# Second layer's edge loop of a two-layer graph network: three small VectorE tensors held in PSUM instead of SBUF

## The reference, cut to what matters

```
W    = (w_comp @ weight.reshape(4, 128*128)).reshape(8, 128, 128)   # 8 types out of 4 bases
proj = einsum('ni,rio->nro', h, W)
msg  = proj[src, rel_type]
agg  = segment_sum(msg, dst)
out  = relu(h @ root_weight + agg + bias);   x = x + out
```

## Time and profile before

| | us |
|---|---|
| median of three runs | 10,770.8 |
| lowest, highest | 10,699.99, 10,827.0 |
| the profiled execution, its own time | 10,833.25 |
| its span, first to last instruction | 10,831.4 |
| PE busy, PEld busy | 6888.0, 5018.6 |
| DVE busy | 4208.4 |
| ACT busy | 958.8 |
| POOL busy | 6283.7 |

### The profile page before, as it was taken

One profiled execution on the slowest core, in us unless ns is written; L12 is line 12 of the kernel. 1 busy time (PEld: TensorE's weight loads), 2 busy tenths in 40 slices (PEclk: granted clock), 3 DMA queues, 4 the chain that ended last, 5 costly groups with the idle time before them and its releaser, 6 DMA issues. The chain is left out here.

```text
span 10831.4 us, 120635 instructions
## 1 busy us (share of the span) xinstructions
PE 6888.0 (64%) x29078; PEld 5018.6 (46%) x29078; DVE 4208.4 (39%) x8057; ACT 958.8 (9%) x1738; POOL 6283.7 (58%) x6284
## 2 busy tenths in 40 slices
PE   5777767777767776667774555565556555555555
PEld 3444444444444444444444444454445444444444
DVE  5444444444444444444453333333333333333333
ACT  2000000010001010001020000000000000000001
POOL 2555555555555555555526666666666666666664
PEclk8777777777777777777786777777777776777777
DMA  5222222222222222222231111111111111111112
GB/s 147 72 72 74 72 72 73 73 72 72 73 71 72 73 73 72 73 73 72 72 84 40 42 39 39 41 41 41 40 39 41 40 39 41 40 39 40 41 40 55
DMA packets 415233, 646.20 MB, mean 60 GB/s; under 512 B 128129, under 2 KB 232009, under 8 KB 414450
## 3 DMA queue, kind: packets, MB, share of 16 engines
q0 software_dynamic: 200704, 411.44, 15.1%
q1 hardware_dynamic: 214482, 234.24, 7.4%
HBM read 617.04 MB, written 28.13 MB: 60 GB/s over the span
## 5 line engine op out<-in xcount | busy, mean ns | idle before, releaser
L559 POOL DMA_INDIRECT G<-p_tab,idxs x3136 | 2981.5, 951 | 2466.7 <-DVE idxs L645 1489.3
L1063 POOL DMA_INDIRECT hT<-h_tab,idxs x3136 | 3300.6, 1052 | 1818.4 <-issue 907.8
L1080 PE MATMUL psA<-S,hT 128*128 128x256 f32 x6272 | 2099.9, 493 | 1811.1 <-DVE S L1150 897.0
L1080 PEld LDWEIGHTS psA<-S,hT 128*128 128x128 f32 x6272 | 1466.0, 246 | 2132.3 <-issue 1055.5
L587 PE MATMUL psM<-Z,w 128*128 128x512 f32 x1568 | 1139.9, 818 | 872.0 <-ACT Z L633 785.6
L662 DVE TENSOR_TENSOR_SCAN R<-mk,R,psM 128x512 f32<-128x512 bf16 x784 | 998.5, 1274 | 1734.2 <-issue 670.2
L1160 DVE TENSOR_TENSOR aggT<-psV,aggT 128x64 f32 x784 | 175.4, 224 | 3319.3 <-remote 1745.0
L603 PE MATMUL psE<-E,O 128*128 128x64 f32 x6272 | 1039.5, 322 | 401.1 <-DVE E L673 329.8
L1090 PEld LDWEIGHTS psV<-A,V 128*128 128x128 f32 x6272 | 1008.0, 231 | 578.2 <-issue 306.6
L1090 PE MATMUL psV<-A,V 128*128 128x64 f32 x6272 | 970.5, 308 | 439.4 <-issue 257.0
L603 PEld LDWEIGHTS psE<-E,O 128*128 128x128 f32 x6272 | 990.6, 240 | 472.3 <-DVE E L673 363.5
(11 more groups left out here) (86 smaller groups left out, 2506.6 us busy)
## 6 DMA issues: line engine op xcount, KB each, us to landing
mk<-marks SPq DMA_DIRECT2D x392, 256.0 KB
G<-p_tab,idxs POOLq DMA_INDIRECT x3136
pl<-marks SPq DMA_DIRECT2D x392, 128.0 KB
hT<-h_tab,idxs POOLq DMA_INDIRECT x3136
Qw<-q_tab SPq DMA_DIRECT2D x784, 32.0 KB
p_tab<-pq SPq DMA_DIRECT2D x14, 448.0 KB, 3.1
q_tab<-pq SPq DMA_DIRECT2D x14, 448.0 KB, 4.1
oh<-in_w SPq DMA_DIRECT2D x392, 4.0 KB
```

The lines of the kernel that those rows point to most:

```text
L559: pool.indirect_dma_start(G[:, s, j, :], None, p_tab, bass.IndirectOffsetOnAxis(ap=idxs[:, s, j:j + 1], axis=0)).then_inc(gathered[s], 16)
L1063: pool.indirect_dma_start(G[:, s, j, :], None, h2_tab, bass.IndirectOffsetOnAxis(ap=idxs[:, s, j:j + 1], axis=0)).then_inc(l1_gathered[s], 16)
L1080: ins = nc.tensor.matmul(psA[:, b, 0:NB * W], G[:, s, j, :], S[:, b, j, :, :].rearrange("p b w -> p (b w)"), start=j == 0, stop=j == GT - 1)
```

## The change

hot, thot and tprod are no longer SBUF tensors of their own. Two PSUM tensors of two banks each are added, so that all eight banks are taken. hot takes the first 256 columns of either bank of psH1, thot the 256 columns behind hot's first buffer, tprod the 1024 columns of psT1. No instruction, no wait and no loop is changed; shapes and types stay (32-bit).

```diff
-                thot = sb("thot", [P, TPI, NR], fp32)
-                tprod = sb("tprod", [P, TPI, NB, NR], fp32)
                 coef = sb("coef", [P, TPI, NB], fp32)
-                hot = sb("hot", [P, 2, GT, W], fp32)
                 S = sb("S", [P, 2, GT, NB, W], fp32)
...
                 psV = ps("psV1", [P, 2, 512])
+                psH = ps("psH1", [P, 2, 512])
+                psT = ps("psT1", [P, 1024])
+                assert GT * W + TPI * NR <= 512 and TPI * NB * NR <= 1024
+                hot = psH[:, :, 0:GT * W].rearrange("p b (j w) -> p b j w", j=GT)
+                thot = psH[:, 0, GT * W:GT * W + TPI * NR].rearrange("p (t r) -> p t r", r=NR)
+                tprod = psT[:, 0:TPI * NB * NR].rearrange("p (t b r) -> p t b r", b=NB, r=NR)
```

## The result

| | before | after |
|---|---|---|
| median, lowest to highest (12 runs each) | 10,770.11, 10,699.99 to 10,827.0 | 10,850.19, 10,835.09 to 10,869.61 |
| ratio after to before, 95% interval | | 1.0088 [1.0067, 1.0108] |
| span of the profiled execution | 10,831.4 | 10,848.1 |
| POOL busy | 6283.7 | 5945.7 |
| second loop in it, first to last of ACT's copies | 5132 | 5221 |

The kernel became slower by 0.9%, 80 us, although POOL has 338 us less to do. In the profiled executions the second loop is 89 us longer.

The account below looks back on a forecast made before the run. No engine fills the second loop: POOL needs 5.41 of 6.56 us a group and otherwise waits for the trailing chain. Profiled 10,833 less 130 gave 10,703, carried over to the runs' median as 10,640 us; range 10,450 to 10,850.

Parts of the forecast that it names:

- POOL's saving: Second loop: S no longer stretches gathers, their mean falls from 1052 to 951 ns, 317 us of POOL time saved.
- bounds 236 and 339: Least and most saving of POOL time in us: the stretch falls on hot as well, or all of it goes.
- priced at nothing: Second loop: hot, still with two SBUF inputs, was taken to add nothing to gathers above 951 ns.
- DVE: Second loop: PSUM operands leave DVE's times about unchanged; effect taken as 0, at most +-25 us.
- What arrives at the end: Second loop: of 317 us saved on POOL, 161 would arrive by the two rates; four fifths, 130 us, was taken.
- two fixed rates: Second loop: the chain passes a group per 7.65 us while POOL issues and per 3.77 us while it stands.
- Slower: Second loop: without S's pauses on POOL the trailing chain slows while POOL issues; 162 us more, 10,933; chance 0.16.
- the 8.3 us beyond which: Second loop: time per group while POOL issues above which the kernel would become slower, a group then costing over 6.51 us.
- The waits: Second loop: POOL's waits for psA and indices, 896 us before, were to become about 1080.
- three sums named beforehand: POOL's waits, second loop: about 1080 us for the forecast, 1210 if nothing arrives, under 900 if all arrives.
- Nothing arrives: Second loop: chain held up once per gather, so POOL's 317 us become stops; 10,771 us; chance 0.26.
- The first loop: It must not move; if it did, the comparison would not be of this change.

Follow-up runs that it names:

- e3: Kernel before with only coef, S's 128-column operand, moved to PSUM; hot, thot, tprod stay in SBUF: 10,963.52 us, 1.0104.
- e1: The change with only hot in PSUM, thot and tprod left in SBUF: 10,971.38 us, 1.0115 to the kernel before.
- e5: The change plus one 384-column POOL memset behind the fourth gather of each second-loop group: 10,690.19 us, 0.9938 to the kernel before.
- f2: The change plus one 384-column POOL memset per group, run again in another comparison: 10,707.34 us, 0.9964 to the kernel before.
- f4: The change plus 384-column POOL memsets behind the second and fourth gather of each group: 10,735.35 us, 0.9879 to the kernel before.
- e4: The change plus a 64-column POOL memset behind each gather of the second loop: 11,051.37 us, 1.0189 to the kernel before.
- x1: The change with the second loop's gathers replaced by POOL memsets to a scratch tensor: 8,463.63 us, beside 10,751.93 of the kernel before.
- x2: The change with the second loop's gathers replaced by SP's plain loads of as many rows, in order: 8,456.88 us, beside 10,751.93 before.
- f3: The change unaltered, run a third time in another comparison: 11,000.17 us, 1.0131 to the kernel before.
- f1: The change unaltered, run again in another comparison: 10,853.37 us, 1.0102 to the kernel before.
- e8: The change plus 384-column POOL memsets behind each group's second and fourth gather, beside a kernel before of 8,599.08 us: 8,738.88 us, 1.0162.
- x3: The change with only the first of each second-loop group's four gathers kept: 8,559.29 us, beside 10,862.99 of the kernel before.

## Why the prediction was wrong

- **POOL's saving: right.** 945 ns in place of a forecast 951, no gather held up by S, 336 us less (317 forecast, bounds 236 and 339). The rule of the Trainium skill (SBUF — State Buffer, Who interferes with whom) that an instruction of DVE with at most one SBUF input does not contend with GpSimd holds, and e3 adds that it holds with the smaller operand in PSUM too. The short instructions with two SBUF inputs hold gathers too, which the forecast priced at nothing. Under hot after the change 188 gathers start and take 966 ns in the mean. Under tprod 97 start: in e1 and e3 all are stretched (1109 ns), and after the change, with thot in PSUM, one is (945 ns in the mean). In the sum this is little.
- **DVE: right.** S 1224 ns, hot 427. The fixed cost of PSUM that the Trainium skill's page VectorE: DVE Perf Modes (The TRN2 errata) gives, by which S would be some 65 ns longer (an estimate from that page), does not show: 1225 and 1224 ns, and 8 ns on hot's write.
- **"What arrives at the end": the step that failed.** It took 7.65 us a group while POOL issues and 3.77 while it stands as two fixed rates, from which each microsecond of issuing saved has to bring something (130 us). Over the whole second loop before the change these rates are 7.56 and 3.97, so they were read rightly; after it they are 8.09 and 4.37, and a group costs 5.00 x (1 - 4.37/8.09) + 4.37 = 6.67 us (5221/784 = 6.66 measured) in place of the 6.31 forecast. The rate while issuing is no constant: after the change it is near 5 us a group for the first 10 us behind a break, then 35 and 14 us (0 copies in the 9.7 us shown). The stretched gathers, by the runs, were themselves breaks. Freed of them, POOL issues 16 gathers on end and has to stop behind each 16. The experiments show the sign: e1 and e3 take POOL's load off and are slower, e5, f2 and f4 give it back in pieces of 0.44 us and are faster. e4, in pieces of 0.17 us, is slower, so it takes a break of some length and not only load; from what length on, no run shows.
- **The rival "Slower": right in its mechanism, its size off.** Its words, the pauses that S forces are the only relief while POOL issues, are what e5 and f4 show. Its price of 162 us was twice the 80 us of the runs. It let a group take 9.18 us while POOL issues, and 8.09 were measured. That is also below the 8.3 us beyond which it was to be the slower case; the kernel was slower all the same, because the rate while POOL stands rose too, from 3.97 to 4.37, which the sum had held fixed.
- **The waits.** Of the three sums named beforehand, 1080, 1210 and under 900 us, none was met: 1262.9 + 47.8 = 1311, past the one at which nothing arrives. The rival "Nothing arrives" falls with that: a chain held up per gather, whatever the time between gathers, would not have run quicker in e5.
- **The Trainium skill's rule that PE and ACT never wait on anyone for SBUF** (SBUF — State Buffer, Who interferes with whom) was taken as speaking for "Nothing arrives". The runs don't contradict it: what comes late is the update of PE's work, and by x1 and x2 neither POOL's writes nor plain transfers slow the chain. No run shows what this rule of the Trainium skill says of SBUF itself.
- **The first loop** was not to move. In the profiles POOL's time in it moved by 72 us (5448 to 5376), and in f3's by 6, so it varies by as much from one execution to the next. The second loop grew in all (5132 before, 5221 after, 5209 in f1, 5297 in f3), which is the sign that was named for a wrong prediction.

What stays open: which part of the chip holds PE's updates back behind indirect DMAs, whether POOL's issuing or the transfers do it, and why in one comparison of the same programs nothing was held back.

## What to carry to other kernels

A saving on an engine that runs ahead of the others can be worth nothing or less; ask what the engine's slow moments let through, and count the rate of the trailing chain by the time since the last break, not only busy against idle. A wait marked "remote", two consumers' work in one burst, and a stop as regular as a clock point to a late signal rather than to a busy engine. Where POOL issues indirect DMAs back to back and the chain behind them shows these marks, a pause of 0.4 us per two gathers is a cheap trial, to be measured against the kernel without it in the same comparison: where nothing was late it cost 1.6% (e8).

## What was not expected of the hardware

- PE's semaphore updates reached ACT and DVE up to 13 us late in the cycle shown, while POOL issued indirect DMAs each 1.25 us, and 2.8 us (median) after its stop; DVE's and ACT's own updates in the same stretch came within 0.01 us. With memsets on POOL, with SP's loads, or with one gather per group, no wait of ACT in the second loop was "remote", and a group took 3.63 us instead of 6.65.
- The granted clock is 0.72 of full speed in the second loop with late updates and 0.91 in x1 to x3, where PE is busy 82 to 83% of the time instead of 58%.
- The same kernel took 8,599 us in one comparison and 10,752 to 10,863 in five others, a fifth less. The four kernels beside it had no late update; that the kernel before had none either is inferred from its time.
- Additional POOL work of 684 us made the kernel 1.2% quicker than the kernel before and 2.4% quicker than the change without it (f4, f3).
